# Attention scores on TensorE: the row maximum from q.k alone in four row groups, the scores for the exponentials as four column tiles of 32 keys

## The reference, cut to what matters

```python
x = x + 0.5 * _L0_ffn_ref(_layernorm(x), ...)
x = x + _L0_attn_ref(_layernorm(x), ...)
x = x + 0.5 * _L0_ffn_ref(_layernorm(x), ...)

# in _L0_attn_ref, H = 16, Dh = 8
attn = jnp.einsum('bhid,bhjd->bhij', q, k) * Dh ** (-0.5)
attn = attn + phi_bias(L)[None, None]      # log(exp(-|pos_i - pos_j|) + 1e-8)
attn = jax.nn.softmax(attn, axis=-1)
out = jnp.einsum('bhij,bhjd->bhid', attn, v)
```

## Time and profile before

| | us |
|---|---|
| median of 3 runs | 1227.99 |
| span of the profiled execution, first to last instruction | 1235.2 |
| attention: first score to last copy of `psV` | 273.4 to 1017.5 |
| steps 1 to 60, start of a step to start of the next | 11.31 each |

### The profile page before, as it was taken

One profiled execution on the slowest core, in us unless ns is written; L12 is line 12 of the kernel. 1 busy time (PEld: TensorE's weight loads), 2 busy tenths in 40 slices (PEclk: granted clock), 3 DMA queues, 4 the chain that ended last, 5 costly groups with the idle time before them and its releaser, 6 DMA issues. The chain is left out here.

```text
span 1235.2 us, 26880 instructions
## 1 busy us (share of the span) xinstructions
PE 1084.3 (88%) x6562; PEld 529.4 (43%) x6563; DVE 933.5 (76%) x1753; ACT 708.5 (57%) x1574; POOL 419.9 (34%) x628
## 2 busy tenths in 40 slices
PE   5549993759999999999999999999999986729997
PEld 4449993422222222222222222222222216629997
DVE  6447774869888888888888888888888817837885
ACT  1024441444777777777777777777777761104443
POOL 2524343443223332323232333323232322642433
PEclk9999997787999999999999999999999996659999
DMA  9221113240111111111111111111111146432221
GB/s 329 97 55 44 41 43 88 96 148 20 30 34 37 32 31 34 36 31 32 35 35 31 31 36 33 31 33 36 32 31 35 28 103 202 164 109 69 67 67 30
DMA packets 54063, 77.03 MB, mean 62 GB/s; under 512 B 15679, under 2 KB 35269, under 8 KB 53368
## 3 DMA queue, kind: packets, MB, share of 16 engines
q1 hardware_dynamic: 48264, 65.25, 18.0%
q0 software_dynamic: 5056, 10.53, 2.3%
q10 hardware_dynamic: 704, 0.79, 0.3%
HBM read 54.61 MB, written 25.41 MB: 65 GB/s over the span
## 5 line engine op out<-in xcount | busy, mean ns | idle before, releaser
L946 DVE TENSOR_REDUCE nmax<-psS 128x1 f32<-128x1024 f32 x512 | 602.9, 1220 | 109.2 <-PE psS L899 109.1
L960 ACT ACTIVATE prob<-psE 128x512 f32<-128x512 f32 x1024 | 537.1, 606 | 179.2 <-PE psE L891 178.9
L899 PE MATMUL psS<-kop,qop 120*128 120x512 bf16 x1024 | 393.8, 388 | 11.6 <-DVE mpart L930 8.6
L891 PE MATMUL psE<-qop,kop 123*128 123x512 bf16 x1024 | 389.1, 382 | 3.4 <-ACT prob L960 2.6
L1004 POOL TENSOR_TENSOR prob<-prob,const 128x512 f32<-128x512 f32 x128 | 162.4, 1269 | 472.5 <-ACT prob L960 472.5
L915 PE MATMUL psV<-prob,vst 128*9 128x512 f32 x2048 | 267.1, 595 | 1.0 <-issue 0.8
L891 PEld LDWEIGHTS psE<-qop,kop 123*128 123x128 bf16 x1024 | 99.3, 98 | 314.1 <-ACT prob L960 219.0
L899 PEld LDWEIGHTS psS<-kop,qop 120*128 120x128 bf16 x1024 | 99.5, 98 | 117.7 <-DVE nmax L946 17.7
L752 ACT ACTIVATE siga<-psGa,w1sa 128x128 f32<-128x128 f32 x156 | 44.5, 368 | 62.9 <-PE psGa L660 62.9
L752 ACT ACTIVATE sigb<-psGb,w1sb 128x128 f32<-128x128 f32 x156 | 44.5, 368 | 60.7 <-PE psGb L660 60.7
L915 PEld LDWEIGHTS psV<-prob,vst 128*9 128x9 f32 x2048 | 30.8, 88 | 109.9 <-issue 109.9
(11 more groups left out here) (163 smaller groups left out, 1023.2 us busy)
## 6 DMA issues: line engine op xcount, KB each, us to landing
qop<-qk_parts SPq DMA_DIRECT2D x192, 48.0 KB
kop<-qk_parts SPq DMA_DIRECT2D x192, 48.0 KB
qk_parts<-part_attend SPq DMA_DIRECT2D x16, 384.0 KB, 2.8
xsb<-sorted_b SPq DMA_DIRECT2D x39, 128.5 KB
weighted_sums<-osum SPq DMA_DIRECT2D x256, 18.0 KB
w1a<-in_w SPq DMA_DIRECT2D x1, 4128.0 KB
w1b<-in_w SPq DMA_DIRECT2D x1, 4128.0 KB
qop<-mrow SPq DMA_DIRECT2D x256, 1.5 KB
```

The lines of the kernel that those rows point to most:

```text
L891: nc.tensor.matmul(psE[BANK[n]][:], kop[b][0:TROWS, kt * P:(kt + 1) * P], qop[b][0:TROWS, cols], start=True, stop=True).then_inc(s_t, 1)
L899: last = nc.tensor.matmul(psS[kt % 2][:, half, :], qop[b][0:SROWS, kt * P:(kt + 1) * P], kop[b][0:SROWS, cols], start=True, stop=True)
L946: nc.vector.tensor_reduce(nmax[r % 2][:, qt:qt + 1], psS[qt % 2][:], AX.XY, ALU.max, negate=True).then_inc(s_max, 1)
L960: nc.scalar.activation(prob[r % 2][:, lo:lo + HALF], psE[BANK[n]][:], ACT.Exp).then_inc(s_exp, 1)
```

## The change

- The score matmuls contract over 32 rows alone, q's and k's leading bf16 parts without the bias. Their operands are new tiles `qS` and `kS` of 128 partitions that hold the 32 rows four times. The four matmuls of two tiles (two query tiles, two halves of the keys) use four row groups of the array, partitions 0, 32, 64, 96.
- Each weigh matmul of 128 keys becomes four of 32 keys in four column groups. The operand has two rows for the maximum in place of three (122 rows). GpSimd splits the maximum in two parts, with 2 instructions in place of 4.
- The order on TensorE in a quarter is now: 2 weighs (8 matmuls), score, score (2 matmuls each), 2 weighs (8 matmuls), gather (8 instructions as before).
- The q and k parts are stored with repetitions, 5 DMAs for q and 6 for k per group of 512 tokens, 128 KB each, in place of 2 of 384 KB. A head is loaded with 4 DMAs (256, 256, 144 and 144 KB) in place of 6 of 48 KB.
- The sums of a head are stored by one DMA of 256 KB (all of `osum`) in place of 4 of 18 KB. `load_sums` has 8 DMAs per sequence in place of 4.

```diff
+TROWS = MAX0 + 2
+QSEQ, KSEQ = "lhhml", "hmlhmh"
+STORES = len(QSEQ) + len(KSEQ)
+SROWS = 4 * DH
...
-                    for z in range(2):
+                    for z, (to, seq) in enumerate(((d.q, QSEQ), (d.k, KSEQ))):
                         sp.wait_ge(s_part, 2 * n + z + 1)
-                        sp.dma_start(d.qk[z, :, b * P:(b + 1) * P, c].rearrange("a p t -> p a t"),
-                                     part[:, n % 2, z, :, :]).then_inc(s_out[n % 2], 16)
+                        for at, a in enumerate(seq):
+                            sp.dma_start(to[b * HEADS:(b + 1) * HEADS, at, :, c],
+                                         part[:, n % 2, z, "hml".index(a), :]).then_inc(s_out[n % 2], 16)
...
 def load_sums(sp, d, g, b):
-    for a in range(2):
...
+    sums = d.sums.rearrange("(b h) (j e) t -> b j h e t", h=HEADS, j=4)
+    for j in range(4):
+        a, half = j // 2, j % 2
+        sp.dma_start(g.den[half * 64:half * 64 + 64, b % 2, a, :],
+                     sums[b, j, :, DH, :].rearrange("h (j q) -> h j q", q=P)).then_inc(g.s_den_in[b], 16)
+        sp.dma_start(g.num[:, b % 2, a, half * HALF:(half + 1) * HALF], sums[b, j, :, 0:DH, :])\
+            .then_inc(g.s_num_in[b], 16)
...
 def load_head(sp, d, g, head, b):
-    for a in range(3):
...
+    def rows(src, at, parts, repeat, step):
+        size = len(QSEQ if src is d.q else KSEQ) * DH * L
+        return bass.AP(tensor=src.tensor, offset=head * size + at * DH * L,
+                       ap=[[step * DH * L, repeat], [L, parts * DH], [1, L]])
+    sp.dma_start(g.qS[b][:], rows(d.q, 0, 4, 4, 0)).then_inc(g.s_op[b], 16)
+    sp.dma_start(g.kS[b][:], rows(d.k, 2, 4, 4, 0)).then_inc(g.s_op[b], 16)
+    sp.dma_start(g.qop[b][0:COMBO, :], rows(d.q, 2, 3, 3, 0)).then_inc(g.s_op[b], 16)
+    sp.dma_start(g.kop[b][0:COMBO, :], rows(d.k, 0, 3, 3, 1)).then_inc(g.s_op[b], 16)
...
+                def weigh(kt):
...
+                        for c in range(4):
                             last = nc.tensor.matmul(
+                                psE[BANK[n]][32 * c:32 * c + 32, :],
+                                kop[b][0:TROWS, kt * P + 32 * c:kt * P + 32 * c + 32],
+                                qop[b][0:TROWS, half * HALF:(half + 1) * HALF], start=True, stop=True)
+                        last.then_inc(s_t, 1)
+                def score(qt):
...
+                    if later(at, 2, 1) or qt >= 2:
+                        pe.wait_ge(s_max, 8 * (i + 2) + qt - 1)
+                    for half in range(2):
+                        lo = 32 * (qt % 2 * 2 + half)
+                        last = nc.tensor.matmul(psS[qt % 2][:, half, :],
+                                                qS[b][lo:lo + SROWS, qt * P:(qt + 1) * P],
+                                                kS[b][lo:lo + SROWS, half * HALF:(half + 1) * HALF],
+                                                start=True, stop=True)
+                    last.then_inc(s_s, 1)
...
+                for p in range(4):
+                    if live(at, 0):
+                        weigh(2 * p)
+                    if live(at, 2):
+                        score(2 * p)
+                        score(2 * p + 1)
+                    if live(at, 0):
+                        weigh(2 * p + 1)
+                    if live(at, -1):
+                        gather(p)
...
-                    nc.gpsimd.tensor_tensor(res[:], nm[:], mp[:, 0, :], ALU.subtract)
-                    pool.drain()
-                    nc.gpsimd.tensor_copy(mp[:, 1, :], res[:])
-                    pool.drain()
-                    nc.gpsimd.tensor_tensor(mp[:, 2, :], res[:], mp[:, 1, :], ALU.subtract).then_inc(s_mp, 1)
+                    nc.gpsimd.tensor_tensor(mp[:, 1, :], nm[:], mp[:, 0, :], ALU.subtract).then_inc(s_mp, 1)
```

More of the change, by code:

```diff
@@ L305, in reciprocals @@
             def reciprocals(b):
-                dve.wait_ge(s_den_in[b], 32)
+                dve.wait_ge(s_den_in[b], 64)
                 if b >= 2:
@@ L850, in step @@
                     sp.wait_ge(s_ev, i - 1)
[L851 to L854, removed]
+                    sp.dma_start(d.sums[bass.ds(i - 2, 1), :, :].squeeze(),
+                                 osum[r % 2][:]).then_inc(s_os[r % 2], 16)
                 if live(at, 1):
@@ L880, in step @@
             def step(i, r, at, q):
[L881 removed]
+                def weigh(kt):
+                    b = r % NBUF
                     for half in range(2):
[L883 to L891, removed]
[L892 to L920 removed]
@@ new lines, in weigh @@
+                        n = 2 * kt + half
+                        if n == 0:
+                            pe.wait_ge(s_mr[b], 64 * filled(q, r, 0))
+                        if later(at, 0, 1) or n >= BANK_AGE[n]:
+                            pe.wait_ge(s_exp, 16 * i + n + 1 - BANK_AGE[n])
+                        for c in range(4):
+                            last = nc.tensor.matmul(
+                                psE[BANK[n]][32 * c:32 * c + 32, :],
+                                kop[b][0:TROWS, kt * P + 32 * c:kt * P + 32 * c + 32],
+                                qop[b][0:TROWS, half * HALF:(half + 1) * HALF], start=True, stop=True)
@@ new lines, in gather @@
+                def gather(p):
+                    if p == 0:
+                        pe.wait_ge(s_vst, i)
+                        if later(at, -1, 1):
+                            pe.wait_ge(s_ev, i - 1)
+                    if p in (0, 2):
+                        pe.wait_ge(s_diag, 2 * i - 1 + p // 2)
+                        pe.wait_ge(s_exp, 16 * i - 8 + 8 * (p // 2))
+                    for j in range(4):
+                        k, half = 2 * p + j // 2, j % 2
+                        last = nc.tensor.matmul(
+                            psV[32 * j:32 * j + VW, :], vst[(r + 1) % 2][:, k, :],
+                            prob[(r + 1) % 2][:, k * PBLK + half * HALF:k * PBLK + (half + 1) * HALF],
+                            start=(p == 0), stop=(p == 3))
+                    if p == 3:
+                        last.then_inc(s_pv, 1)
@@ L1068, in build @@
             g.kop = [am.sb(f"kop{n}", [TROWS, L], BF16) for n in range(NBUF)]
+            g.qS = [am.sb(f"qS{n}", [P, L], BF16) for n in range(NBUF)]
+            g.kS = [am.sb(f"kS{n}", [P, L], BF16) for n in range(NBUF)]
             g.s_op = [am.sem(f"s_op{n}") for n in range(NBUF)]
@@ L1104 @@
     qbias = np.zeros((6, KT, L), bf16)
-    kbias = np.zeros((6 * KT + 3, L), bf16)
+    kbias = np.zeros((6 * KT + 2, L), bf16)
     for t in range(KT):
@@ L1112 @@
             kbias[(3 + a) * KT + t] = np.where(tile == t, part.astype(np.float32), np.float32(0)).astype(bf16)
-    kbias[6 * KT:] = np.ones((3, L), bf16)
+    kbias[6 * KT:] = np.ones((2, L), bf16)
     const = np.zeros((P, C_END), np.float32)
```

70 lines of the change are left out of this document (18 added, 52 removed).

## The result

The kernel after takes 1289.36 us, the median of 4 runs (1282.53 to 1292.38); beside them the kernel before took 1228.42 (1227.91 to 1229.41). The ratio is 1.0497, with a 95% interval of 1.0464 to 1.0529: slower by 61 us. The prediction was 1165 with a range of 1138 to 1216, a faster kernel; the sign is wrong.

A forecast was written before the change was run, and what follows sets the result against it. TensorE was taken as the bound, at 11.31 us a step. Steps 1 to 60 -69.6, "attend" +5.3, steps 61 to 63 +1.4, step 63 -0.8, "last" +1.0 sum to -62.7: from 1228.0 to 1165 us, range 1138 to 1216.

The forecast's parts named there:

- The wait of the second pair: On TensorE, the second score pair waits for the previous quarter's second reduction: 0.1 us per quarter.
- the halves of the loop: TensorE's quarter as the mean of two stretches between score pair starts, 2.86 and 2.20 us: 2.53.
- the term of -69.6: Steps 1 to 60 of the attention: each falls from 11.31 to 10.15 us, -69.6 us together.
- What hides the rest: Other engines and DMAs in a step: 1.06 MB takes 4.6 us of 10.15 at 228 GB/s, hidden, at zero.
- Phase attend: The phase "attend" ends with SP's last store, later because of more stores: +5.3 us.
- The count alone decides: In "attend", the number of SP's DMAs sets the added time, so never less than the +5.3 us taken.
- Steps 61 to 63, the end: Attention's end and phase "last": +1.4 us from more loads on SP, -0.8 in step 63, +1 in "last".
- Rival 4: In the steps, maxima land after the head's 1.06 MB at 105 GB/s, a step of 12: about 1225 us; chance 0.04.
- Rival 3: On TensorE, narrow weighs are issue-bound, 0.43 us a group, a step of 11.83: slower, 1266 us; chance 0.10.
- rival 1: In the steps, VectorE becomes the bound, a step of 9.64 us, -100 in place of -69.6: 1135 us; chance 0.10.
- rival 2: On TensorE, tiles overlap only in part or geometry changes cost more; without overlap a step of 11.0, 1216 us; chance 0.23.
- Rival 5: TensorE's clock falls; half the time at the low level gives about 1290 us; chance 0.03.

The follow-up runs named there:

- e1: The changed kernel with each head's four loads cut into 14 DMAs with partitions outermost, same bytes: 1212.98 us, ratio 0.9788 to the kernel before.
- e6: e1 with 72 stores in place of 88 and heads 0 to 2 loaded by four DMAs each: 1186.66 us, ratio 0.9658 to the kernel before.
- e5: The changed kernel with the maxima's four DMAs issued by GpSimd in place of SP, loads unchanged: 1207.64 us, ratio 0.9839 to the kernel before.
- e2: The changed kernel's loads and stores with the kernel before's TensorE order, row-group scores and column tiles undone: 1293.3 us, ratio 1.044 to the kernel before.

## Why the prediction was wrong

*What bounds the kernel; the change on TensorE.* Right. Weigh groups are 0.22 (0.22 to 0.43 was the range), four scores take 0.45 with a change (0.44 + 0.12 predicted), changes cost about 0.1. The wait of the second pair, the loop's one non-trivial element, is in e1's trace with 0.17, and the halves of the loop are 2.16 and 2.83 where 2.20 and 2.86 were predicted. (The prediction calls 2.20 the stream per quarter; that is a slip of words, since it holds one score pair.) A step was predicted at 10.15 and takes 10.3 where nothing else disturbs it. What is missing is at the head's start: 0.29, the exponential on the same bank. With a step of 10.3 the term of -69.6 would have been -61.

*"What hides the rest": the step that failed.* It took 105 GB/s at a DMA share of 46%, scaled it to 228 at full use, and so priced 1.06 MB at 4.6 us, "hidden, at zero". The scaling presumes that every DMA is spread over all engines. The new loads have an outermost dimension of four or three; their traffic is 10.1 us on three engines, and the maxima, issued behind them on the same queue, land 6.6 after their issue. The term was zero and is 11.97 - 10.30 = 1.67 us per step, 100 us in all, of which 76 are waits for the maxima and 24 go with the low clock. (Steps 1 to 60 missed their forecast by 39.7 + 69.6 = 109; the other 9 are the head's start.) The trace of before gave a hint. Its loads have an outer dimension of three, and in windows over them alone the share is 0.12 to 0.17:

```profile
507.50:509.00 1.50, 1.50 (x12) 0.33 (x11) 1.50 (x2) 1.31 (x3) 0.54 (x3) 1.00 0.12 41
509.00:510.50 1.50, 1.50 (x8) 0.49 (x5) 1.15 (x3) 1.42 (x3) 0.00 (x0) 1.00 0.17 61
```

It was a hint and no proof, since the issues explain this rate as well: 48 KB every 0.90 us are 55 GB/s. At that rate 800 KB of loads take longer than a step; at after's 98 GB/s they take 8. The number to scale was that of the loads themselves, not that of a stretch in which other DMAs ran.

*"Phase attend".* Wrong by 18.7 of 24.0, in two ways. The size: a store was taken at 0.42 with its gap and is 0.65; its pattern in DRAM changed too, and that this is the reason wasn't tested. With 0.65 the two groups and the loads between them, counted as the prediction did, take 22 x 0.65 + 2.9 = 17.2 in place of 7.0, +10.2. The count: the other 13.8 are SP's backlog from the earlier groups. 66 us of issues don't fit into the 47 in which the stores of before were done, so the phase was bound by SP throughout, not at its end alone. "The count alone decides" was right, but was applied to the last two groups only. e6 shows it from the other side: 16 stores and the cut loads fewer, and 16 us came back.

*Steps 61 to 63, the end.* +1.4 predicted and +0.7 measured for steps 61 and 62, -0.8 and +0.6 for the end, +1 and -1.4 for the phase "last". All small. The end is 14.2 in e1, 0.6 less than in before, as good as predicted; after ran it with a granted clock of 0.89 behind a wait of 2.02 for the maxima.

*The rivals.* Rival 4 was the one that came true: maxima that land after the head's traffic, with a step of 12. It named a rate (105 GB/s, near the 98 measured), not the reason, the few engines. It had a chance of 0.04, and its time was put at 1225, between its two ends; its own step of 12 gives 60 x 0.69 + 7 = 1276, and with "attend" as it was, 1295. The chance was so low only because of the 228 GB/s. Rival 3 (narrow weighs bound by issue) is excluded by the 0.22 steps, rival 1 by the 10.3 of e1, and rival 2, whose 11.0 is 11.03 by its own terms (1218 and not 1216), by e1 too. Rival 5: the clock does fall, but after the waits; in e1, with the densest stream, the undisturbed windows are at 1.00. The low clock accounts for some 24 us in all and comes after waits.

*The direction of the idea was right.* With the DMAs arranged so that they hide (e6), the kernel gets 3.4% faster, where 5.1% was predicted; of the 22 us between the two, 16 are "attend", 84.7 against 68.7.

What is open: whether e5's maxima pass the loads on the same engines or run on others, and what exactly in the store's pattern costs SP 0.60 and not 0.37; another arrangement of the same bytes wasn't tried. That the alternation of steps comes from the lead that a wait gives to the next loads is read from one pair of steps and not tested.

## What to carry to other kernels

Read a DMA's rate from windows in which that kind of DMA runs alone: a share that stands at 0.25 or 0.20 while such loads are queued means four or three engines of 16, and then the traffic must be divided by those, not by 16. A low share may also come from slow issues (e1, and the loads of before), so compare the bytes of a DMA with the time from one issue to the next. A small DMA that an engine waits for should not stand behind such loads on the same queue: spread them with partitions outermost, or give the small one another engine's queue (e5). When a change multiplies the DMAs of a phase, count SP's issues over the whole phase against its length, and take their duration from a DMA of the same pattern.

## What the runs showed of the hardware

- Loads with an outer dimension of four or three copies move 99 and 76 GB/s at a share of 0.26 and 0.20, as much as four and three of 16 engines give at 84 ns per packet of 2048 bytes. Cut into DMAs with 32 or 24 partitions outermost, the same rows have a share of 0.50 and 139 GB/s, and there the issues set the rate.
- The maxima's DMAs, issued by GpSimd while SP's queue is full of such loads, land in 2.2 us (median, e5); issued behind the loads on SP's own queue they took 6.6 in the step shown. On which engines they ran isn't shown.
- What a DMA costs its issuer depends on its form: 0.35 for `weighted_sums<-osum` (256 KB), 0.43 for a piece of 32 partitions in e1 (1.73 for four, in the same timeline), 0.60 for a store of 128 KB whose side in DRAM has three dimensions, 0.61 to 0.78 for the loads with copies, 0.56 for a small one from GpSimd.
- Four bf16 matmuls in four row groups of 32 run side by side (0.51 from the start of the first to the end of the last, one alone 0.39), as do four in four column groups, which step by 0.22. From weighs to gathers, both in column groups, no gap is seen; to and from the scores it is about 0.1.
- A pause of 2.65 on TensorE was followed by some 3.5 us at a granted clock of 0.54, though the engine streamed almost without a gap in them (3.48 of 3.50 busy). In after such falls follow the waits of most second steps, 2.0 to 2.9 long, and one of 1.6; in e2, with waits of up to 1.8, the clock doesn't fall. So these runs give no sharp line between them.
